# Turning the second layer's input: sixteen on-chip transfers and VectorE block turns in place of TensorE turns

## The reference, cut to what matters

```
def gat_layer(x, W, adj):
    Wh, Ws = split(x @ W, 2, axis=-1)
    a = softmax(Wh @ Ws.T, axis=-1) * adj
    return leaky_relu(a @ Wh + x, 0.01)
x1  = gat_layer(x, W_stack[0], adj)
x2  = gat_layer(x1, W_stack[1], adj)
out = layernorm(x + x2)
```

## Time and profile before

| | |
|---|---|
| median of three runs | 476.89 us |
| the profiled execution's own time | 477.23 us |
| its span | 475.4 us |
| granted clock of TensorE over the span | 0.998 |
| PE busy | 463.0 us (97%) |
| DVE busy | 372.1 us (78%) |
| ACT busy | 232.3 us (49%) |
| POOL busy | 190.6 us (40%) |
| shares of the chain that ended last | PE 87%, DVE 7%, issue 2%, DMA 2% |

### The profile page before, as it was taken

How to read it: one execution, slowest core, us unless ns; L and a number is a source line. 1 busy time by engine, 2 the same in 40 slices (tenths; PEclk the granted TensorE clock), 3 DMA queues, 4 the chain that set the end, 5 groups by cost and what they waited for, 6 DMA issues and landing times.

```text
span 475.4 us, 5636 instructions
## 1 busy us (share of the span) xinstructions
PE 463.0 (97%) x1854; PEld 304.2 (64%) x1854; DVE 372.1 (78%) x832; ACT 232.3 (49%) x411; POOL 190.6 (40%) x186
## 2 busy tenths in 40 slices
PE   8999999999999999999999999899999999999993
PEld 6999745545555588877544444454557546778882
DVE  4688799999998599739236757998755698799984
ACT  5979529980889653323334532251332475342200
POOL 1444665631425058823001541361430064456641
PEclk9999999999999999999999999999999999999999
DMA  8856310000364100000000000000000000000001
GB/s 280 284 181 193 123 40 0 1 1 0 117 193 161 32 0 1 0 1 1 1 0 0 0 1 1 1 0 1 0 1 0 1 1 1 0 13 22 23 22 40
DMA packets 8180, 20.68 MB, mean 44 GB/s; under 512 B 1008, under 2 KB 4740, under 8 KB 8152
## 3 DMA queue, kind: packets, MB, share of 16 engines
q1 hardware_dynamic: 7144, 19.02, 12.3%
q0 software_dynamic: 464, 0.79, 0.7%
q10 hardware_dynamic: 544, 0.52, 0.3%
HBM read 18.94 MB, written 1.39 MB: 43 GB/s over the span
## 4 chain that ended last, share of the span: by engine, by line
PE 87%; DVE 7%; issue 2%; DMA 2%; SPq 1%; ACT 1%; POOLq 0%; POOL 0%; DVEq 0%
PE psum L1544 19%; PE psum L1359 11%; PE psum L1335 11%; PE psum L1581 9%; PE psum L1644 8%; PE psum L1316 6%; PE psum L1422 6%; PE psum L1524 4%; PE psum L1237 2%; PE psum L1497 2%; PE psum L1379 2%; PE psum L1615 2%; PE psum L1406 2%; DMA adj_rows<-in_adj_dram 2%; PE psum L1476 1%
## 5 line engine op out<-in xcount | busy, mean ns | idle before, releaser
L1544 PE MATMUL psum<-QT,xT 128*128 128x512 f32 (+3 forms) x264 | 108.3, 542 | 1.7 <-ACT ST L634 1.7
L440 POOL TENSOR_TENSOR es<-es,ST 128x512 f32<-128x512 f32 (+3 forms) x60 | 74.9, 1248 | 53.8 <-ACT ST L639 52.1
L634 ACT ACTIVATE ST<-psum 128x512 f32<-128x512 f32 (+3 forms) x66 | 36.1, 546 | 89.6 <-DVE rm L994 77.9
L1544 PEld LDWEIGHTS psum<-QT,xT 128*128 128x128 f32 (+1 forms) x264 | 48.1, 186 | 44.5 <-issue 38.2
L994 DVE TENSOR_TENSOR rm<-psum,rm 128x512 f32<-128x512 f32 (+3 forms) x60 | 37.4, 624 | 41.2 <-PE psum L1544 41.0
L376 POOL TENSOR_TENSOR rstd<-veps,nhalf 128x1 f32<-128x1 f32 (+1 forms) x44 | 29.4, 668 | 65.0 <-DVE veps L770 65.0
L1644 PE MATMUL psum<-Wh,ST 128*128 128x256 f32 (+3 forms) x242 | 55.1, 380 | 0.0
L1581 PE MATMUL psum<-ST,Wh 128*128 128x512 f32 (+3 forms) x132 | 53.9, 542 | 0.0
L404 POOL TENSOR_TENSOR esumb<-esumb,eb 128x1354 f32<-128x1354 f32 (+1 forms) x10 | 34.5, 3447 | 46.4 <-ACT eb L528 46.4
L1359 PE MATMUL psum<-eb,x_all 128*128 128x512 f32 (+3 forms) x132 | 51.8, 542 | 0.0
L1335 PE MATMUL psum<-adjT,x_all 128*128 128x512 f32 (+3 forms) x132 | 50.1, 542 | 0.0
(11 more groups left out here) (181 smaller groups left out, 781.7 us busy)
## 6 DMA issues: line engine op xcount, KB each, us to landing
adj_rows<-in_adj_dram SPq DMA_DIRECT2D x10, 677.0 KB, 5.2
rows<-in_adj_dram SPq DMA_DIRECT2D x10, 677.0 KB, 4.0
x_all<-in_x_dram SPq DMA_DIRECT2D x5, 256.0 KB, 4.5
out_dram<-xs SPq DMA_DIRECT2D x10, 128.0 KB, 1.7
W<-in_L_gnn_W_stack_dram SPq DMA_DIRECT2D x2, 512.0 KB, 6.4
adj_rows<-in_adj_dram SPq DMA_DIRECT2D x1, 338.5 KB
rows<-in_adj_dram SPq DMA_DIRECT2D x1, 338.5 KB
w0n<-in_L_gnn_weight_dram SPq DMA_DIRECT2D x1, 256.0 KB, 2.8
```

Of the source, the lines that this page charges most:

```text
L440: nc.gpsimd.tensor_tensor(es[0:r, g % 2, 0:w], es[0:r, g % 2, 0:w], buf(g)[0:r, j, 0:w], ALU.add)\
L1544: last = nc.tensor.matmul(psum[0:r, SB[n % 3], 0:w], xT[l][:, k, j * P:j * P + r], QT[:, k, c0:c1], start=(k == 0), stop=(k == KD - 1))
```

## The change

x1 in natural layout is no longer made by TensorE and ScalarE: `turn_x1` and `x1_copy` and their semaphores are gone, and so are their two banks of PSUM traffic. Instead:

1. SP waits for all three chunks of `xT[1]`, and issues 16 transfers from SBUF to SBUF. The transfer (a, b) takes partitions 32b to 32b+31 of `xT[1]` and, of each block of 128 columns, the 32 columns from 32a on, and puts them in partitions 32a to 32a+31 of `x1blocks`. Each run is 32 values, 128 bytes; a transfer has 32 partitions with 2 x 11 runs each, 704 runs. `x1blocks` lies over `xT[0]`, so it is also under `ST2`.
2. VectorE turns 32 x 32 blocks from `x1blocks` to `x1a` and `x1b`, in six instructions (`x1_blocks`): two of 128 x 512 after the stage of group 4's score tiles, two of 128 x 512 after `run_max(5, 0)`, two of 128 x 384 after `soft_step(4, 1)`.
3. `st_copy(5, 0)` on ScalarE waits for the last of the six.
4. GpSimd zeroes the padding columns of `xT[1]` (54 of each 1408) once, after the third layer's norms.

```diff
+        x1blocks = at("x1blocks", SLOT, [P, KD, T, QUADS, BLOCK])
...
+            sp.wait_ge(x1_pads.sem, 1)
+            sp.wait_ge(xT1_ready.sem, NC)
+            for a in range(QUADS):
+                for b in range(QUADS):
+                    sp.dma_start(x1blocks[a * BLOCK:(a + 1) * BLOCK, :, :, b, :],
+                                 xT[1][b * BLOCK:(b + 1) * BLOCK, :, :].rearrange("u k (i a v) -> u k i a v", a=QUADS, v=BLOCK)[:, :, :, a, :])\
+                        .then_inc(x1_in.sem, 16)
...
+            nc.gpsimd.memset(xT[1][:, :, N:NP], 0.0).then_inc(x1_pads.sem, 1)
...
                 if j == 0 and g == G - 1:
-                    act.wait_ge(xT1_ready.sem, NC)
+                    act.wait_ge(x1n_ready.sem, T)
...
-            def x1_copy(i):
-                r = kk(i)
-                act.wait_ge(x1_turned.sem, i + 1)
-                if i == 0:
-                    act.wait_ge(wh1_done.sem, T)
-                    act.wait_ge(qT_ready.sem, KD * G)
-                nc.scalar.activation(x1n(i)[0:r, :], psum[0:r, XB[i % 3], 0:D], ACT.Copy).then_inc(x1n_ready.sem, 1)
...
+            def x1_blocks(i0, i1, k):
+                if i0 == 0:
+                    dve.wait_ge(x1_in.sem, 16 * QUADS * QUADS)
+                    dve.wait_ge(wh1_done.sem, T)
+                if i0 == CROSS:
+                    dve.wait_ge(qT_ready.sem, KD * G)
+                home = x1a[:, i0:i1, :] if i0 < CROSS else x1b[:, i0 - CROSS:i1 - CROSS, :]
+                last = nc.vector.transpose(home[:, :, k * P:(k + 1) * P], x1blocks[:, k, i0:i1, :, :].rearrange("p i b v -> p i (b v)"))
+                if k == KD - 1:
+                    last.then_inc(x1n_ready.sem, i1 - i0)
...
             for s in range(T):
                 both(3, s)
+            for k in range(KD):
+                x1_blocks(0, EB, k)
             max_reduce(4)
             run_max(5, 0)
+            for k in range(KD):
+                x1_blocks(EB, CROSS, k)
             run_max(5, 1)
             soft_step(4, 0)
             soft_step(4, 1)
+            for k in range(KD):
+                x1_blocks(CROSS, T, k)
...
-            def turn_x1(i):
-                r = kk(i)
-                pe.wait_ge(xT1_ready.sem, NC)
-                if i == 0:
-                    pe.wait_ge(wh1_ready.sem, T)
-                    pe.wait_ge(qT_ready.sem, KD * G)
-                if i >= 3:
-                    pe.wait_ge(x1n_ready.sem, i - 2)
-                for k in range(KD):
-                    last = nc.tensor.transpose(psum[0:r, XB[i % 3], k * P:(k + 1) * P],
-                                               xT[1][:, k, i * P:i * P + r], ident[:, :])
-                last.then_inc(x1_turned.sem, 1)
...
             for j in range(T):
                 s_tile(4, j)
                 if j == 0:
                     wh1(T - 1)
-                else:
-                    turn_x1(j - 1)
-            turn_x1(T - 1)
             sum_n(0, 0, 2)
             max_turn(4)
```

More of the change, by code:

```diff
@@ L220, in gnn_stack @@
         adj_in_tail = sem("adj_in_tail")
+        x1_in, x1_pads = sem("x1_in"), sem("x1_pads")
         rows2_in = [sem("rows2_in_even"), sem("rows2_in_odd")]
@@ L273, in gnn_stack @@
         rden_ready, rdb_ready = sem("rden_ready"), sem("rdb_ready")
-        wh1_done, wh1_ready, x1_turned, x1n_ready, out_ready = (
-            sem("wh1_done"), sem("wh1_ready"), sem("x1_turned"), sem("x1n_ready"), sem("out_ready"))
+        wh1_done, wh1_ready, x1n_ready, out_ready = (
+            sem("wh1_done"), sem("wh1_ready"), sem("x1n_ready"), sem("out_ready"))
         NG = Norm("gat")
@@ L703, in _ @@
                     wh1_evac(T - 1)
-                else:
-                    x1_copy(s - 1)
-            x1_copy(T - 1)
             st_copy(5, 0)
@@ L1637, in sum_n @@
                     pe.wait_ge(gat_read.sem, NC + max(i - 2, 0))
-                if i <= 2 and j0 == 0:
-                    pe.wait_ge(x1n_ready.sem, T - 2 + i)
+                if i == 0 and j0 == 0:
+                    pe.wait_ge(wh1_ready.sem, T)
+                    pe.wait_ge(qT_ready.sem, KD * G)
                 for j in range(j0, j1):
```

## The result

| | median of the runs | runs | profiled execution | its span | granted clock, mean |
|---|---|---|---|---|---|
| before | 477.15 us (476.69 to 478.52) | 7 | 477.23 us | 475.4 us | 0.998 |
| after | 479.71 us (478.71 to 480.61) | 7 | 478.84 us | 477.0 us | 0.997 |

The account below looks back on a forecast made before the run. TensorE and VectorE were both taken as full, with the start of `max_turn(5)` deciding. The stage's -0.48 is eaten by later waits, turns and gate add 0.9: 476.89 + 0.9 = 477.8 us, range 475.7 to 479.8.

Parts of the forecast that it names:

- the gate: `st_copy(5, 0)` waits for the block turns until 407.07; group 4's first exponential comes 1.4 us later.
- one collision: At `norm_n(0)`, GpSimd's late tile 3 addition holds one of its two-SBUF-operand operations until about 414.5: +0.9 us.
- rival 4: The gate costs more, by a second collision or slower turns: +2 to +3, 479.4 us, chance 0.11.
- +0.9: Turns and gate together at `max_turn(5)`, the net change to the whole time; bounds of the term -1.1 and +2.0.
- TensorE's 2.4 us: All 22 turns and copy-related gaps removed from TensorE; it would stand idle for what it could not gain.
- 1.88 us a tile: Pace of the 380 to 400 us stage, set by VectorE and GpSimd excluding each other, in place of 1.935.
- The term of -0.48: 380 to 400 us stage: `run_max(4, 10)` 0.48 us sooner, at 399.16; bounds 0 and 1.2.
- GpSimd's one memset: Lies where GpSimd waits for ScalarE; priced at nothing.
- Block turns: Six on VectorE, 3.46 us in all, mostly in its 4.2 us free from 400 to 410 us.
- The transfers: SP's 16 issues at 0.50 us, some 20 ns a run, in at 380 us, hidden: cost nothing.
- rival 3: Transfers late, a run costing over 46 ns; at 60 ns VectorE stalls 9 us, end 485; chance 0.10.
- 1 and 2: Rivals: VectorE not made late, 475.8 us, chance 0.20; TensorE's 2.4 us come through whole, 474.5, chance 0.06.

Follow-up runs that it names:

- e1: Kernel before without TensorE's 22 turns and ScalarE's 11 copies, nothing in their place: 476.40 us, ratio 0.9977.
- e5: Kernel before plus only the change's memset of the padding columns on GpSimd: 477.04 us, ratio 0.9997.
- e6: Changed kernel with the padding memset on VectorE instead of GpSimd: 479.60 us, ratio 1.0054.
- e3: Changed kernel with the wait for the block turns moved from `st_copy(5, 0)` to `st_copy(5, 5)`: 477.26 us, ratio 0.9995.
- e4: Changed kernel with group 4's first two exponentials put ahead of `st_copy(5, 0)` and `st_copy(5, 1)` on ScalarE: 476.79 us, ratio 0.9991.
- e2: Kernel before with `st_copy(5, 0)` on ScalarE held until group 4's second subtraction: 478.58 us, ratio 1.0028.
- e9: Changed kernel with the second operand of `norm_n(0)`'s two operations read from PSUM instead of SBUF: 477.75 us, ratio 1.0006.
- e11: Changed kernel with SP's 16 transfers held back until group 3's eighth subtraction: 482.36 us, ratio 1.0118.
- e8: Changed kernel, gate at `st_copy(5, 5)`, group 4's last two maxima before group 3's last two multiplications, first four block turns after `run_max(5, 0)`: 476.01 us, ratio 0.9973.
- e10: e8 with the padding memset on VectorE instead of GpSimd: 475.89 us, ratio 0.9968.

## Why the prediction was right, and which term was mis-sized

The forecast was slower, by the gate and one collision, and so it went. That the range of 475.7 to 479.8 holds the median of 479.71 is partly luck: it does so by 0.09, three of the seven runs lie outside, and the forecast's own range of 476.9 to 478.8 is missed. By the time alone one would have taken the result for rival 4 (479.4). +0.9 was too small: the interval of 1.4 to 2.9 us leaves it out. Another 0.26 of the distance from 477.8 to 479.71 is the base, the median of three runs (476.89) where that of seven is 477.15.

1. **TensorE's 2.4 us do not come through.** Right. It waits 1.86 us before `max_turn(4)` (1.6 forecast) and 1.91 before `max_turn(5)` (1.9). e1 shows what they are worth without the rest: -1.1 us in time, 0.46 at `run_max(4, 10)`.
2. **1.88 us a tile.** Right as a pace: (399.71 - 384.68) / 8 = 1.879. **The term of -0.48 failed all the same.** The first two tiles take 0.39 us longer (4.90 against 4.51), and the eight after them 0.45 less: `run_max(4, 10)` is at 19.93 against 19.99. The step that failed is "GpSimd's one memset lies where GpSimd waits for ScalarE; nothing". The memset itself is hidden. But with it GpSimd's first addition of group 3 starts 0.43 to 0.46 us after its copy, not 0.14, and that decides which multiplication is caught. e5 shows it in the kernel before, e6 takes it out of the one after: 19.54, and +1.05 at `max_turn(5)` in place of +1.45. Why an instruction 154 us earlier moves that gap is open; no run separates the memset from the semaphore that it raises.
3. **Block turns.** Six in 1.29 + 1.28 + 1.03 less overlaps, 3.4 us against 3.46, in the free time of 400 to 410. Right.
4. **The gate.** Right in kind: the copy starts at 407.85 (407.07 forecast; 0.55 of the difference is there at `run_max(4, 10)`, 399.71 against 399.16), released by a block turn, and the exponentials at 408.51. e3 and e4 take it away by two means and land on the same 49.17. e2 puts the delay alone into the kernel before and costs 1.10.
5. **The collision with `norm_n(0)`.** Right in place, a little small: 1.45 against 0.42 is 1.03, where I had 0.9; e9 gives back 1.04. From the anchor, `norm_n(0)` starts 0.43 late (413.77 - 379.78 = 33.99, before 413.21 - 379.65 = 33.56): 0.43 + 1.03 = 1.46, the whole +1.45. The 0.43 is the stage's missing gain: with it (e6) `norm_n(0)` starts 414.31 - 380.71 = 33.60 after the anchor, and the collision alone is left, +1.05.
6. **The transfers.** Hidden, as forecast. SP took 11.74 / 16 = 0.73 us an issue, not 0.50; a run of 128 bytes took 0.503 x 16 x 17 us / 11520 = 12 ns, not 20. The last issue starts at 376.8, and with the median of 2.6 it has landed at about 379.4, near the 380 of the forecast, by two errors that cancel; VectorE asks at 400.91. e11 shows what the cover is against. The Trainium skill, "DMA: Bandwidth & Descriptors", section "Why small descriptors are slow (HBM only)", says that transfers from SBUF to SBUF don't suffer the penalty of small pieces; that was the rule for this case, not the one that rival 3 took from the section "Specifications". The trace agrees so far that 12 ns is nowhere near the 86 of a doubled 1 KB price. But for each byte these runs still took about twice as long as the 1 KB packets of the earlier trace rows (12 ns for 128 bytes, 43 for some 900), so no run here shows small pieces to be free.
7. **Rivals.** 1 and 2 are out (later, not sooner), and 3 by point 6. Rival 4, "the gate costs more", gave +2 to +3 by a second collision; the runs show one collision of 1.03, and 0.4 from the stage. The traces' +1.45 to +1.61 is in the lower part of the times' 1.4 to 2.9. The runs' mean granted clocks bear on the surplus: the three runs of the changed kernel at 0.996 or 0.997 took 478.71 to 478.84, the four at 0.993 or 0.994 took 479.71 to 480.61, and of 35 runs of the kernel before the 20 at 0.996 or more took 476.44 to 477.61, median 477.07. At like clocks the change costs 478.77 - 477.07 = 1.7, close to the traces. Why four of these seven runs had the lower clock isn't shown; the kernel before has such runs too, 478.11 to 478.94 at 0.992.

## What to carry to other kernels

When two engines are both full, taking work from one is worth only the distance to the other: compute the second's pace, with its collisions, first. When an edit adds a wait, put it no earlier than at the first instruction that needs it (e3 wins back 1.84 us in the trace by moving the gate five tiles on), and look at what is queued behind it rather than at the instruction itself. Then use the freed time by reordering: the change as made costs 2.1 us, with the gate and the maxima moved (e8) it saves 1.3, and with the memset on VectorE as well (e10) 1.5.

## What the runs showed of the hardware that I had not expected

- One memset more on GpSimd, 154 us earlier, lengthens the gap between its copy and its next addition from 0.14 to 0.43 us (e5) and 0.46 (after). Moved to VectorE it is 0.14 again (e6, e10).
- A `tensor_scalar` with one SBUF input is held by a GpSimd addition (1.32 us), and takes 0.29 us when free; a `scalar_tensor_tensor` with one SBUF and one PSUM input is not held (0.42 us during the addition).
- In e11 TensorE stood idle for 2.82 us up to 405.79, after a wait of 1.86 that ended at 399.90. The granted clock was 1.00 in 403 to 405, then 0.86, 0.50 (1.2 GHz of 2.4) in 407 to 409 and 0.79: it fell after work had begun again (1.00 still in 405.8 to 406.2, 0.50 in 406.6 to 407), and was back at 1.00 from 410. In the changed kernel, after waits of 1.86 and 1.91 us, it stayed 1.00.
